# Distance attention in a fused decoder: scores of two heads in two row halves, query norms as a matmul of their own, row sums inverted on VectorE

## What is computed

```
P = X @ W_in + b_in                 # 16 heads, each with Q, K, V, G of 64
d2 = sum(Q*Q)[:, None] + sum(K*K)[None, :] - 2 * Q @ K.T
W = (1e-4 + sqrt(max(d2, 0))) ** -2
W = W / (1e-4 + sum(W, axis=-1, keepdims=True))
H = G * (W @ V)
out = H @ W_out + b_out             # heads side by side
```

## Time and profile before

| what | before |
|---|---|
| median of three runs | 1385.69 us |
| profiled execution, time | 1387.55 us |
| its span in the trace | 1385.7 us |
| TensorE busy | 1263.2 us (91%) |
| VectorE busy | 987.1 us (71%) |
| ScalarE busy | 929.9 us (67%) |
| GpSimd busy | 507.5 us (37%) |

### The profile page before, as it was taken

How to read it: one execution, slowest core, us unless ns; L and a number is a source line. 1 busy time by engine, 2 the same in 40 slices (tenths; PEclk the granted TensorE clock), 3 DMA queues, 4 the chain that set the end, 5 groups by cost and what they waited for, 6 DMA issues and landing times.

```text
span 1385.7 us, 17134 instructions
## 1 busy us (share of the span) xinstructions
PE 1263.2 (91%) x6134; PEld 697.4 (50%) x6134; DVE 987.1 (71%) x1816; ACT 929.9 (67%) x1200; POOL 507.5 (37%) x359
## 2 busy tenths in 40 slices
PE   6999999999999999988888888999899999977666
PEld 3455544444554445423222225777666776853444
DVE  7777777667777677657889882456468767758895
ACT  3999999999999998945677764455455445523321
POOL 2444444444444444754556430233200000025333
PEclk9999999999999999977999997999999999989777
DMA  8200000000000000100000000000100000000000
GB/s 178 61 1 1 0 0 1 0 0 1 1 1 0 0 1 1 62 1 16 1 0 1 2 0 1 0 1 1 57 1 1 1 0 1 1 1 1 0 8 23
DMA packets 27711, 15.01 MB, mean 11 GB/s; under 512 B 16638, under 2 KB 26476, under 8 KB 27500
## 3 DMA queue, kind: packets, MB, share of 16 engines
q1 hardware_dynamic: 27628, 13.92, 3.8%
HBM read 12.86 MB, written 1.05 MB: 10 GB/s over the span
## 4 chain that ended last, share of the span: by engine, by line
PE 78%; DVE 12%; issue 5%; POOL 2%; ACT 2%; DMA 0%; POOLq 0%; SPq 0%; ACTq 0%; DVEq 0%
PE PS L1854 16%; PE PS L1863 8%; DVE ARENA L977 5%; PE PS L850 4%; PE PS L1835 4%; PE PS L1169 4%; PE PS L833 4%; PE PS L754 3%; PE PS L1177 2%; PE PS L705 2%; PE PS L1200 2%; PE PS L721 2%; PE PS L1880 2%; PE PS L1192 2%; PE PS L1823 2%
## 5 line engine op out<-in xcount | busy, mean ns | idle before, releaser
L2216 DVE TENSOR_SCALAR ARENA<-PS,ARENA 128x512 f32<-128x512 f32 x256 | 189.9, 749 | 57.2 <-PE PS L1854 38.6
L1854 PE MATMUL PS<-ARENA 128*128 128x512 f32 x512 | 227.4, 597 | 3.1 <-issue 2.3
L2352 POOL TENSOR_TENSOR ARENA<-ARENA 128x1024 f32<-128x1024 f32 x64 | 151.0, 2360 | 126.6 <-ACT ARENA L2044 122.0
L977 DVE TENSOR_REDUCE ARENA<-PS 128x1 f32<-128x512 f32 x256 | 161.0, 681 | 32.5 <-PE PS L721 32.1
L895 ACT ACTIVATE ARENA<-PS 128x1024 f32<-128x1024 f32 x128 | 128.3, 1025 | 49.7 <-PE PS L740 49.6
L1854 PEld LDWEIGHTS PS<-ARENA 128*128 128x128 f32 x512 | 95.6, 191 | 115.1 <-issue 112.4
L2028 ACT ACTIVATE ARENA<-ARENA 128x2048 f32<-128x2048 f32 x64 | 122.2, 1911 | 33.6 <-DVE ARENA L2216 33.2
L2036 ACT ACTIVATE ARENA<-ARENA,consts_sb 128x2048 f32<-128x2048 f32 x64 | 127.7, 1996 | 0.4
L1863 PE MATMUL PS<-ARENA 128*64 128x512 f32 x512 | 118.4, 605 | 0.9 <-DVE ARENA L2216 0.9
L2044 ACT ACTIVATE ARENA<-ARENA 128x2048 f32<-128x2048 f32 x64 | 118.3, 1896 | 0.0
L2194 DVE TENSOR_SCALAR ARENA<-PS,BT 64x512 f32<-64x512 f32 x64 | 48.0, 749 | 79.2 <-PE PS L1835 75.6
(11 more groups left out here) (258 smaller groups left out, 2595.3 us busy)
## 6 DMA issues: line engine op xcount, KB each, us to landing
ARENA<-in_window_bias_dram SPq DMA_DIRECT2D x1, 1536.0 KB, 6.7
WKVG<-in_L_attn_W_in_dram SPq DMA_DIRECT2D x3, 448.0 KB, 6.9
X<-in_x_dram SPq DMA_DIRECT2D x4, 256.0 KB, 5.0
W<-in_L_ffn_w_dram SPq DMA_DIRECT2D x1, 1024.0 KB
out_dram<-X SPq DMA_DIRECT2D x4, 256.0 KB, 2.2
WQ<-in_L_attn_W_in_dram SPq DMA_DIRECT2D x2, 448.0 KB, 8.4
BV<-in_L_attn_b_in_dram SPq DMA_DIRECT2D x1, 512.0 KB, 6.5
Wout<-in_L_attn_W_out_dram SPq DMA_DIRECT2D x1, 512.0 KB, 4.7
```

Source lines behind the costliest of these rows:

```text
L977: dve.tensor_reduce(NMX[:, w % 2, t, h:h + 1], bank(("cS", n, j)), AX.X, ALU.max, negate=True).then_inc(sem("c_max"), 1)
L1854: done(pe.matmul(o, SK[:, hd, kt * P:(kt + 1) * P], MQ[:, hd, :], start=True, stop=True), ("S", u, c))
L2216: dve.tensor_scalar(D[:, u % 2, hd, kt, :], bank(("S", u, c)), K2[:, u % 2, kt, hd:hd + 1], 1e-30, ALU.add, ALU.max).then_inc(sem("guarded ...
L2352: pool.tensor_tensor(WPAIR, D[:, u % 2, hd, 0:2], D[:, u % 2, hd, 2:4], ALU.add).then_inc(sem("w_paired"), 1)
```

## The change

- The two heads of a pair share one buffer each for keys and queries, head 0 in rows 0 to 63 and head 1 in rows 64 to 127. A score matmul has 64 rows, and successive ones alternate between the two row halves. D is ordered by key tile and then by head, and ScalarE's two halves are now key tiles 0, 1 and 2, 3 with both heads.
- The query norms are computed once for a pair, by a matmul of the squares with the constant `pairsum` (`query_norms`), scaled by -0.5 on VectorE into `QX`, and added to each score tile by an fp32 matmul of 32 rows whose weights (`FIRST`) are one in the first row and zero in the others. The four tiles of a half take four row groups. These matmuls open the accumulation and the scores close it.
- Queries are projected once for a pair. Keys and queries are made two units ahead, values and gates one unit ahead.
- Row sums of u-2 come between the two score halves of u. The 1e-4 is added by a bf16 matmul of 32 rows (three bf16 pieces of the number); VectorE inverts the sum with one RECIPROCAL of 128x512 (`inverse`) between guards 3 and 4, and `gated(u-2)` follows guard 7.
- ScalarE's squares and its logarithm and exponential of the row sums are gone. GpSimd adds in three operations of 128x1024 in place of two of 128x1024 and two of 128x512.
- Pool "A" has six banks and the weighted values one of their own (pool "PV"), which is read by `gated`.
- Buffers: MQ and SK have slots for even and odd units, the query weights are loaded once, and a few small buffers lie in memory that others use at another time. In the stage behind the loop the row sums of unit 30 come at step 1 and their inverse at step 3, those of unit 31 at steps 9 and 11.

The core of the diff (removed function bodies that the listing above shows are left out, as are constants, small buffers and the tail's calls):

```diff
-POOLS = {"all": range(BANKS), "A": range(0, 7), "out0": range(7, 8), "cS": range(0, 3), "cV4": range(3, 4), "cP": range(4, 8)}
+POOLS = {"all": range(BANKS), "A": range(0, 6), "PV": range(6, 7), "out0": range(7, 8), "cS": range(0, 3), "cV4": range(3, 4), "cP": range(4, 8)}
...
-        D, at = carve(0, [2, 2, QT, S])
+        D, at = carve(0, [2, QT, 2, S])
...
-                for half in range(2):
-                    sp.dma_start(WQ[:, heads, half, :], w_in[:, 0, heads]).then_inc(sem(name), 16)
+                sp.dma_start(WQ[:, 0, heads], w_in[:, 0, heads]).then_inc(sem(name), 16)
...
+            def project_pair(u):
                 b, p = divmod(u, PAIRS)
                 o = begin(("K", u))
                 done(pe.matmul(o, wpair(p, 0), XT[:, b], start=True, stop=True), ("K", u))
+                o = begin(("Q", u))
+                w = WQ[:, 0, 2 * p:2 * p + 2, :].rearrange("p h e -> p (h e)")
+                done(pe.matmul(o, w, XT[:, b], start=True, stop=True), ("Q", u))
...
-                for hd, key in ((0, "QA"), (1, "QB")):
-                    o = begin((key, u))
-                    w = WQ[:, 2 * p + hd].rearrange("p a e -> p (a e)")
-                    done(pe.matmul(o, w, XT[:, b], start=True, stop=True), (key, u))
...
+            def query_norms(u):
+                pe.wait_ge(sem("qsq"), u + 1)
+                o = begin(("q2", u))
+                done(pe.matmul(o, const("pairsum"), QSQ, start=True, stop=True), ("q2", u))
...
-            def scores(u):
-                pe.wait_ge(sem("mq_scaled"), 2 * u + 2)
-                pe.wait_ge(sem("mq_squared"), 2 * u + 2)
-                pe.wait_ge(sem("k_sb"), 2 * u + 2)
-                for c in range(8):
-                    hd, kt = divmod(c, QT)
-                    o = begin(("S", u, c))
-                    done(pe.matmul(o, SK[:, hd, kt * P:(kt + 1) * P], MQ[:, hd, :], start=True, stop=True),
+            def scores(u, half):
+                if half == 0:
+                    pe.wait_ge(sem("q2_sb"), u + 1)
+                    pe.wait_ge(sem("mq_scaled"), u + 1)
+                    pe.wait_ge(sem("k_sb"), u + 1)
+                banks = {}
+                for c in range(4 * half, 4 * half + 4):
+                    g = slice(32 * (2 * (c % 2) + c // 2 % 2), 32 * (2 * (c % 2) + c // 2 % 2) + 32)
+                    banks[c] = begin(("S", u, c))
+                    pe.matmul(banks[c], FIRST[g, :], QX[g, u % 2, :], start=True, stop=False)
+                for c in range(4 * half, 4 * half + 4):
+                    kt, hd = divmod(c, 2)
+                    r = slice(64 * hd, 64 * hd + 64)
+                    done(pe.matmul(banks[c], SK[r, u % 2, kt * P:(kt + 1) * P], MQ[r, u % 2, :], start=False, stop=True),
                          ("S", u, c))
...
+            def row_sums(u):
+                pe.wait_ge(sem("w_summed"), u + 1)
                 o = begin(("RS", u))
                 for hd in range(2):
+                    pe.matmul(o[hd * 64:hd * 64 + 64, :], EPSW[0:32, :], PIECES[0:32, 0:1].to_broadcast([32, S]),
+                              start=True, stop=False)
+                for hd in range(2):
                     mm = pe.matmul(o[hd * 64:hd * 64 + 64, :], const("ones")[:, 0:64], WSUM[:, u % 2, hd, :],
-                                   start=True, stop=True)
+                                   start=False, stop=True)
                 done(mm, ("RS", u))
...
             for u in range(UNITS):
-                scores(u)
+                scores(u, 0)
+                if u >= 2:
+                    row_sums(u - 2)
+                scores(u, 1)
                 if u == 0:
-                    pe.wait_ge(sem("win_in"), 16 * 5)
+                    pe.wait_ge(sem("win_in"), 16 * 4)
+                    project_pair(1)
+                    query_norms(1)
+                    key_norms(1)
+                if u + 2 < UNITS:
+                    project_pair(u + 2)
                 if u + 1 < UNITS:
-                    project_keys(u + 1)
+                    project_values_and_gates(u + 1)
                 if u >= 1:
                     weighted_values(u - 1)
-                if u + 1 < UNITS:
-                    project_queries(u + 1)
-                    key_norms(u + 1)
+                if u + 2 < UNITS:
+                    query_norms(u + 2)
+                    key_norms(u + 2)
...
-                    if hd == 0 and u >= 1:
-                        row_sums(u - 1)
-                    if hd == 0 and u + 1 < UNITS:
-                        squares(u + 1)
...
+            def evacuate_pair(u):
                 p = u % PAIRS
                 full(dve, ("K", u))
+                dve.tensor_scalar(SK[:, u % 2, :], bank(("K", u)), BKP[:, p:p + 1], None, ALU.add
+                                  ).then_inc(sem("k_sb"), 1)
+                full(dve, ("Q", u))
+                dve.tensor_scalar(MQ[:, u % 2, :], bank(("Q", u)), BQP[:, p:p + 1], -2.0, ALU.add, ALU.mult
+                                  ).then_inc(sem("mq_scaled"), 1)
+                dve.wait_ge(sem("k_sb"), u + 1)
+                dve.tensor_tensor(KSQ, SK[:, u % 2, :], SK[:, u % 2, :], ALU.mult).then_inc(sem("ksq"), 1)
+                dve.wait_ge(sem("mq_scaled"), u + 1)
+                dve.scalar_tensor_tensor(out=QSQ, in0=bank(("Q", u)), scalar=BQP[:, p:p + 1], in1=MQ[:, u % 2, :],
+                                         op0=ALU.add, op1=ALU.mult).then_inc(sem("qsq"), 1)
...
+            def query_norms(u):
+                full(dve, ("q2", u))
+                if u >= 2:
+                    full(dve, ("S", u - 2, 7))
+                dve.tensor_scalar(QX[:, u % 2], bank(("q2", u)), -0.5, None, ALU.mult).then_inc(sem("q2_sb"), 1)
+            def inverse(u):
+                full(dve, ("RS", u))
+                if u >= 1:
+                    dve.wait_ge(sem("gr"), u)
+                dve.reciprocal(RR, bank(("RS", u))).then_inc(sem("rs_inv"), 1)
...
             for u in range(UNITS):
                 for c in range(4):
-                    if c == 0 and u >= 2:
-                        full(dve, ("RS", u - 2))
                     guard(u, c)
+                if u >= 2:
+                    inverse(u - 2)
                 for c in range(4, 8):
                     guard(u, c)
+                if u >= 2:
+                    gated(u - 2)
+                if u == 0:
+                    evacuate_pair(1)
+                    query_norms(1)
+                    key_norms(1)
+                if u + 2 < UNITS:
+                    evacuate_pair(u + 2)
                 if u + 1 < UNITS:
-                    evacuate_keys(u + 1)
-                    evacuate_queries(u + 1)
-                if 1 <= u < UNITS - 1:
-                    gated(u - 1)
-                if u + 1 < UNITS:
+                    evacuate_values(u + 1)
                     evacuate_gates(u + 1)
-                    key_norms(u + 1)
+                if u + 2 < UNITS:
+                    query_norms(u + 2)
+                    key_norms(u + 2)
...
+                pool.wait_ge(sem("w_ready"), 2 * u + 1)
+                if u >= 2:
+                    full(pool, ("RS", u - 2))
+                pool.tensor_tensor(WSUM[:, u % 2], D[:, u % 2, 0], D[:, u % 2, 1], ALU.add).then_inc(sem("w_paired"), 1)
+                pool.wait_ge(sem("w_ready"), 2 * u + 2)
+                if u:
+                    pool.wait_ge(sem("w_summed"), u)
+                pool.tensor_tensor(WPAIR, D[:, u % 2, 2], D[:, u % 2, 3], ALU.add).then_inc(sem("w_paired"), 1)
+                pool.wait_ge(sem("w_paired"), 2 * u + 2)
+                pool.tensor_tensor(WSUM[:, u % 2], WSUM[:, u % 2], WPAIR, ALU.add).then_inc(sem("w_summed"), 1)
...
-                if u >= 1:
-                    scale_gates(u - 1)
                 sum_weights(u)
                 if u in (29, 30):
                     stack(pool, u - 29)
+                scale_gates(u)
...
```

More of the change, by code:

```diff
@@ L72, in constant_columns @@
         cols[f"{name}_drops_mid"] = (which == 2).astype(np.float32)[:, None]
+    piece = part % 32
+    cols["is_first"] = (piece == 0).astype(np.float32)[:, None]
+    cols["is_piece"] = (piece < 3).astype(np.float32)[:, None]
+    cols["eps_piece"] = np.zeros((P, 1), np.float32)
+    rest = np.float32(EPS0)
+    for i in range(3):
+        high = ((np.array(rest, np.float32).view(np.uint32) + np.uint32(0x8000)) & np.uint32(0xffff0000)).view(np.float32)
+        cols["eps_piece"][piece == i] = high
+        rest = np.float32(rest - high)
     cols["eps_w"] = np.full((P, 1), EPS0)
@@ L160, in cross_out_job, with weighted_values_job, row_sums_job, ahead @@
     return [(("xo", b), 1, [("x_new", stream_no(1, b))], pool)]
-def weighted_values_job(u, pool, sums_pool):
-    return [(("PV", u), 1, [("h_done", u + 1)], pool), (("RS", u), 1, [("rs_log", u + 1)], sums_pool)]
+def weighted_values_job(u, pool):
+    return [(("PV", u), 1, [("h_done", u + 1)], pool)]
+def row_sums_job(u, pool):
+    return [(("RS", u), 1, [("rs_inv", u + 1)], pool)]
```

(42 more changed lines are left out.)

152 lines of the change are left out of this document (81 added, 71 removed).

## The result

The changed kernel takes 1423.36 us (median of 4 runs, 1421.01 to 1430.55) against 1384.95 for the kernel before: 1.029 times, 95% interval 1.024 to 1.033; ratios here and below are of means, so they differ a little from the quotient of two medians. The profiled execution took 1425.44 us, its span 1423.6, so 38 us more than the profiled execution before.

The account below looks back on a forecast made before the run. TensorE bound the loop before; after, the order through VectorE's reciprocal would, at 18.9 us a unit. Loop 36.5, unit 31 3.6, start 3.5 and tail 4 add 47.6 us: 1433 us median, range 1385 to 1480 (about 0.8).

Parts of the forecast that it names:

- Reciprocal: VectorE, between guards 3 and 4: 512 elements in a row take 3.36 us, bounds 0.75 and 4 us.
- fp32 row groups: TensorE's norm matmuls: four groups overlap fully; rivals, partial overlap 1473 us (chance 0.04), none 1640 us (0.03).
- TensorE's own work: Loop unit on TensorE: 36.5 slots, 15.67 us, plus nine tile-shape changes, 1.1 to 2.0 us: 16.7 to 17.6 us.
- The first rival: Loop: reciprocal takes only 0.75 us, weighted values never wait, TensorE binds at about 16.7 us: 1363 us, faster; chance 0.13.
- The break-even of 2.1 us: Loop: reciprocal length at which the change would neither gain nor lose, 3.36 - 1.26 us.
- The chain through the unit: Loop: norms, guards, reciprocal, guards, gated, weighted values, norms and output in order take 18.9 us a unit, against 17.62.
- The second wait: Loop: TensorE idle 0.4 us ahead of the queries, besides 1.2 us ahead of the weighted values.
- The sum: Whole kernel: 36.5 for 29 intervals, 3.6 for unit 31, 3.5 at the start, 4 behind the loop: 47.6 us more.
- Start: Units 0 and 1: unit 0 takes 5.2 us more, unit 1 1.7 us less; together 3.5 us more.
- Behind the loop: Stage after the loop: two reciprocals in VectorE's busy queue replace ScalarE's passes, 2 to 6.7 us, taken as 4.
- The clock in the loop: Rival: TensorE's idle time lowers its clock; a tenth of the loop at 1.2 GHz gives 1480 us, a fifth 1530; chance 0.07.
- (D): Rival theory in the experiments, not the prediction: the change's new order of banks causes the loss; no size or chance given.

Follow-up runs that it names:

- the run with the short inversion: Changed kernel with VectorE's 128x512 reciprocal replaced by one tensor_scalar of the same shape, about 0.7 us, sums not inverted: 1389.62 us, 1.0052 to the kernel before.
- the run with the late reciprocal: Changed kernel with the reciprocal moved behind guard 7, directly ahead of gated: 1579.25 us, 1.1422 to the kernel before.
- the fastest kernel: Changed kernel with ScalarE's inversion, no addend matmuls, key squares from PSUM, query norms added in VectorE's guards, no clamp: 1329.97 us, 0.9629 to the kernel before.

## Why the prediction was right, step by step

1433 was predicted for the median, 1423 was measured. The likeliest case is the one that came, by the mechanism given: a reciprocal of 3.4 us in the middle of the guards, and TensorE waiting behind it. But the terms missed on both sides, the loop by 15 us too many and the stretch behind it by 8.5 too few, so that the total came out within 10 us is in part luck.

- **Reciprocal.** 3.36 us from the line through four short rows, 3.35 measured on 512 elements; the 4.3 us set against it did not come. It decided the sign, and the run with the short inversion shows that: 1390.
- **fp32 row groups.** Full overlap was taken; 1.14 us for eight records in four row groups, 3.70 in one.
- **TensorE's own work.** 16.7 to 17.6 us; it was 17.4 to 17.5 (nine changes of at most 0.2 each, (17.51 - 15.67) / 9), near the upper end. The first rival, 16.7, was therefore priced too low: a short inversion gives 1390, not 1363. With that, the rival was no gain at all. The break-even of 2.1 us goes by the loop alone; start, unit 31 and the stretch behind the loop, 11 us in the prediction's own sum, are not in it.
- **The chain through the unit.** 18.9 us predicted, 18.41 measured. The steps by the trace, counted from 227.14: first guard 2.3 (2.3 predicted); guard 3 done 5.1 (5.4), since four guards end 0.66 us apart and not 0.765, a distance I had taken from a row that held two instructions of another shape; reciprocal done 8.3 (8.7); guards done 10.9 (11.8); gated done 11.5 (12.5); weighted values 11.6 (12.6). TensorE stood only 0.31 us ahead of them, not 1.2.
- **The second wait.** 0.4 us ahead of the queries was predicted and 0.36 ahead of their norms came, but from a cause that the prediction lacked: it gave the squares 0.75 us, and the key squares took 2.16 beside GpSimd. Ahead of the queries themselves there was no wait: they start 0.97 us after the keys with the reciprocal and without it. Guards too slow by 1 us and squares too fast by 1.4 partly cancelled. Of the 0.90 us that the reciprocal costs a unit, the chain that the prediction wrote down gave 0.47, and the collision of the squares, which it did not have, 0.43: this is the other piece of luck.
- **The sum.** 29 intervals: 36.5 predicted, 21.5 measured (18.88 against 18.14 each, and 18.41 against 17.62 in plain units). Unit 31: 3.6 predicted, 0.9 measured. Start: 3.5 and 3.7. Behind the loop: 4 predicted, 12.5 measured.
- **Behind the loop** is the term most wrong for its size. I had priced two reciprocals in VectorE's queue at 2 to 6.7 us; they cost 9.5. And I had nothing for the rest of the change, which costs 3.0:

```profile
625.93 0.63 PE L1923 MATMUL PS<-PIECES,EPSW 32*64 32x512 bf16 x2 [2.41 <-POOL ARENA L2422]
...
659.76 0.61 PE L779 MATMUL PS<-ARENA 32*128 32x512 bf16 x2 [4.08 <-DVE ARENA L2244]
```

```profile
656.36 3.35 DVE L2244 RECIPROCAL ARENA<-PS 128x512 f32<-128x512 f32 x1
```

  The row sums of unit 30 wait for GpSimd's third add, the scores of the stage behind wait 4.08 us for the second reciprocal, and the granted clock from 621 to 693 us is 0.69; before, it was 0.74 over the 60 us from the stage's start. With the short operation the first of these waits is gone, the second is 1.41 us and the clock is 0.78, and 9.5 of the 12.5 us come back. How they split between the waits and the clock was not tested.
- **The clock in the loop** stayed at 1.00; that rival didn't come here. It came in the run with the late reciprocal, where TensorE stands 4.16 us at a stretch.

What stays open: (D) was not undone by itself. It is bounded by the run with the short inversion, 1.0052 in all, start and tail included; the one effect of the banks that was seen in the loop is the wait in the second norm group, at most 0.11 us a unit in the changed kernel. Whether ScalarE or TensorE holds the fastest kernel at 15.6 us is open too.

## What to carry to other kernels

Count an instruction's cost by what is queued behind it on its engine: a 3.35 us operation on an engine that is busy 84 and 88% of the loop cost 2.2% alone in the kernel before and 2.4% in the changed one (1.0288 against 1.0052), in two quite different orders. Look, too, at what it pushes together on other engines: nearly half of its price in the changed loop was a collision that it had moved. When a matmul is halved, count what is needed to make the halves fit, in the same slots: 8 slots went, and 4 slots of norm matmuls and seven more changes of tile shape took nearly all of it back, while a second addend in a VectorE operation that reads PSUM anyway was free. And before time is taken out between two halves that share banks, see whether the banks are back by then; if not, put work there instead.

## What the runs showed of the hardware

- VectorE's RECIPROCAL took 202, 256, 353 and 428 ns for 8, 16, 32 and 44 elements in a row and 3346 ns for 512, from PSUM: 6.2 to 6.3 ns an element.
- A VectorE product with both inputs in SBUF took 2.16 us beside GpSimd's adds, 0.98 where it met them for 0.43 us, and 0.75 with one input in PSUM. In the first two cases GpSimd's next add took 2.70 and 2.68 us, in the third 2.37.
- Four fp32 matmuls of 32 rows in four row groups: 1.14 us for eight records; in one group 3.70.
- A wait of TensorE for a bank within a group of matmuls shows as a longer group (1.58 against 1.15 us) and not as idle time: "busy 500 of 500" did not mean that its own work was the bound.
- After 4.16 us of idle time the next two groups of matmuls took 1.82 and 1.92 us against 1.02 and 1.05, at a granted clock of 0.66 from 216 to 221 us.
- With all norm matmuls in one row group TensorE was busy without a break and was granted 0.90 of its clock from 60 to 597 us; with four row groups and the short inversion, busy 533 of 537 us, it was granted 1.00. The first is a single execution, and the cause is open.
